# Turning rows feature-major with VectorE in 32x32 blocks, from a quarter-wise DRAM layout, in place of TensorE transposes

## The reference

```
ys = cond / sqrt(512)                                  # (2, 512), one row per batch
d  = rsqrt((ys*ys) @ (weight*weight) + 1e-8)
xf = ((x * ys[:, None, :]) @ weight) * d[:, None, :]   # (4096, 512)
top1   = argmax(softmax(xf @ gate_w.T))                # expert 0 or 1 for each token
shared = relu(xf @ sw1 + sb1) @ sw2 + sb2              # hidden size 2048
routed = sum over e of (relu((xf * onehot_e) @ w1[e] + b1[e]) @ w2[e] + b2[e])
out    = x + routed + shared
```

## Time and profile before

| | |
|---|---|
| median of 3 runs | 1588.66 us |
| profiled execution, span from first to last instruction | 1588.7 us |
| PE busy | 1577.0 us (99%) |
| DVE, ACT, POOL busy | 630.3, 348.1, 156.9 us (40%, 22%, 10%) |
| granted TensorE clock, mean | 0.996 of full speed |
| DMA | 105.65 MB, 67 GB/s in the mean |
| `rows` load of 1 MB (L338, L316), issue to landing | 7.0 us median of 8 |
| xf store of 256 KB (L304), issue to landing | 2.0 us median of 32 |

### The profile page before, as it was taken

One profiled execution on the slowest core, in us unless ns is written; L12 is line 12 of the kernel. 1 busy time (PEld: TensorE's weight loads), 2 busy tenths in 40 slices (PEclk: granted clock), 3 DMA queues, 4 the chain that ended last, 5 costly groups with the idle time before them and its releaser, 6 DMA issues.

```text
span 1588.7 us, 23419 instructions
## 1 busy us (share of the span) xinstructions
PE 1577.0 (99%) x8516; PEld 1365.6 (86%) x8516; DVE 630.3 (40%) x1349; ACT 348.1 (22%) x644; POOL 156.9 (10%) x204
## 2 busy tenths in 40 slices
PE   8999999999999999999999999999999999999998
PEld 7878888888888888888889999999999999999997
DVE  6885532323232323323257333333337333333333
ACT  3443211111111111111134111111125111111112
POOL 0000620000000000000010111111111111110112
PEclk8999999999999999999999999999999999999999
DMA  5655230202010020202034111110016111000111
GB/s 187 218 184 168 85 95 14 93 13 92 13 61 31 13 92 13 92 13 80 14 126 146 33 40 40 40 40 26 26 44 206 40 40 40 30 24 26 40 40 43
DMA packets 51458, 105.65 MB, mean 67 GB/s; under 512 B 6433, under 2 KB 6945, under 8 KB 51425
## 3 DMA queue, kind: packets, MB, share of 16 engines
q1 hardware_dynamic: 41888, 77.90, 14.8%
q0 software_dynamic: 9536, 27.32, 5.6%
HBM read 79.48 MB, written 26.25 MB: 67 GB/s over the span
## 4 chain that ended last, share of the span: by engine, by line
PE 97%; issue 1%; DMA 0%; DVE 0%; POOLq 0%; POOL 0%; ACT 0%; DVEq 0%; ACTq 0%; SPq 0%
PE h_ps L1074 45%; PE y_ps L1091 44%; PE h_ps L1007 6%; PE t_ps L1053 2%; PE h_ps L981 0%; POOLq L422 0%; DMA res<-partial_scratch,idx_res 0%; PE y_ps L996 0%; PE y_ps L1159 0%; DMA stage<-w_pack 0%; PE t_ps L987 0%; PE y_ps L987 0%; POOL out L444 0%; PE t_ps L1194 0%; PE h_ps L1133 0%
## 5 line engine op out<-in xcount | busy, mean ns | idle before, releaser
L1074 PE MATMUL h_ps<-x_hi,w_hi 128*128 128x256 f32 (+1 forms) x1536 | 488.6, 318 | 1.6 <-DVE x_lo L739 1.5
L1074 PE MATMUL h_ps<-x_hi,w_lo 128*128 128x256 f32 (+1 forms) x1536 | 489.0, 318 | 0.0
L1074 PE MATMUL h_ps<-x_lo,w_hi 128*128 128x256 f32 (+1 forms) x1536 | 488.9, 318 | 0.0
L563 ACT ACTIVATE hf<-h_ps,b 128x256 f32<-128x256 f32 (+1 forms) x384 | 210.3, 548 | 1116.8 <-PE h_ps L1074 1116.6
L903 DVE CAST h_hi<-hf 128x256 fp32r<-128x256 f32 (+1 forms) x384 | 134.3, 350 | 806.0 <-ACT hf L563 804.5
L1091 PE MATMUL y_ps<-w_hi,h_hi 128*128 128x512 f32 x1024 | 404.0, 395 | 0.0
L1091 PE MATMUL y_ps<-w_lo,h_hi 128*128 128x512 f32 x1024 | 400.9, 392 | 0.0
L1091 PE MATMUL y_ps<-w_hi,h_lo 128*128 128x512 f32 x1024 | 398.7, 389 | 0.0
L1074 PEld LDWEIGHTS h_ps<-x_hi,w_hi 128*128 128x128 f32 x1536 | 291.7, 190 | 32.3 <-issue 2.2
L1074 PEld LDWEIGHTS h_ps<-x_lo,w_hi 128*128 128x128 f32 x1536 | 291.8, 190 | 28.8 <-issue 0.2
L1074 PEld LDWEIGHTS h_ps<-x_hi,w_lo 128*128 128x128 f32 x1536 | 291.7, 190 | 20.0
(11 more groups left out here) (132 smaller groups left out, 733.8 us busy)
## 6 DMA issues: line engine op xcount, KB each, us to landing
stage<-w_pack SPq DMA_DIRECT2D x96, 256.0 KB, 2.8
res<-x_cols SPq DMA_DIRECT2D x32, 256.0 KB, 2.8
xf_scratch<-hf SPq DMA_DIRECT2D x32, 256.0 KB, 2.0
rows<-xf_scratch SPq DMA_DIRECT2D x8, 1024.0 KB, 7.0
res<-x_rows SPq DMA_DIRECT2D x8, 1024.0 KB, 5.3
scratch<-w_pack SPq DMA_DIRECT2D x16, 512.0 KB, 3.6
partial_scratch<-res SPq DMA_DIRECT2D x32, 256.0 KB, 2.2
rows<-w_cond SPq DMA_DIRECT2D x4, 256.0 KB, 4.7
```

Source lines behind the costliest of these rows:

```text
L563: nc.scalar.activation(hf[:, j % 2, 0:tok], h_ps[j % 2][:, 0:tok], ACT.Relu, bias=b1[:, ffn, j:j + 1]).then_inc(hf_ready, 1)
L1074: last = nc.tensor.matmul(h_ps[j % 2][:, 0:tok], lhs[:, j, part], rhs[:, k, 0:tok], start=(k == 0 and q == 0), stop=(k == KD - 1 and q == 2))
```

## The change

`xf_dram` now has four times as many rows of 128 features: row q * 4096 + t has, of token t, block q of each of the four 128-feature pieces (the columns of the projection's weights and of the gate's are reordered on the host, so the kernel's own result comes out in this order). `rows` is filled so that 32 partitions hold quarter q and each partition has 32-token blocks behind one another: a wide slot takes four loads of 32 partitions, a narrow slot eight indirect DMAs of 128 rows of 512 bytes instead of two of 2048 bytes. VectorE turns all 32x32 blocks in place with one transpose instruction (`flip`: 128 x 2048 elements for a wide slot, 128 x 1024 for a narrow one), after step j = 13 of the slot ahead, after quad 2 in a short slot, and in the prologue ahead of the last round of tiles. ScalarE and VectorE then make `x_hi` and `x_lo` from `rows` in SBUF. All transposes at L1053 and L1180 are gone. A second table of token numbers, with q * 4096 added, is read by four DMAs of 32 partitions. What frees `rows` for the next load or gather is now `x_lo` (`xt_lo`) and no longer the transpose (`xt_ps`).

```diff
@@ layout and loads
-    xf_dram = nc.dram_tensor("xf_scratch", (N, D), F32).ap()
+    xf_dram = nc.dram_tensor("xf_scratch", (QD * N, QF), F32).ap()
-        rows = sb("rows", [P, M, D])
+        rows = sb("rows", [P, JW, QF])
-                    sp.dma_start(token_rows(xf_dram, c * P, P), xo[:, i % 2, :]).then_inc(xf_out[i % 2], DMA)
+                    sp.dma_start(quads_of(c * P, P), xo[:, i % 2, :].rearrange("p (q f) -> p q f", q=QD)).then_inc(xf_out[i % 2], DMA)
-                sp.wait_ge(xt_ps, KD * (s + 1))
-                sp.dma_start(rows[:], slot_rows(xf_dram, s + 1)).then_inc(rows_in, DMA)
+                sp.wait_ge(xt_lo, KD * (s + 1))
+                for q in range(QD):
+                    sp.dma_start(rows[q * B32:(q + 1) * B32, :, :], quad_rows(q, s + 1)).then_inc(rows_in, DMA)
@@ GpSimd
+                for q in range(QD):
+                    pool.dma_start(tab_rows[q * B32:(q + 1) * B32, :],
+                                   table_dram.rearrange("(c p) w -> p c w", p=B32)[:, :, 0]).then_inc(tab_dma, DMA)
-                wait_apart(pool, xt_ps, until(s, NARROW, KD, KD // 2), tab_ready)
-                numbers(idx_rows, tab_in, s)
-                for m in range(ME):
-                    pool.indirect_dma_start(rows[:, m, :], None, xf_dram,
-                                            bass.IndirectOffsetOnAxis(idx_rows[:, m:m + 1], 0)).then_inc(rows_gathered, DMA)
+                wait_apart(pool, xt_lo, until(s, NARROW, KD, KD // 2), tab_ready)
+                numbers(idx_rows, tab_rows, s, JN)
+                for j in range(JN):
+                    pool.indirect_dma_start(rows[:, j, :], None, xf_dram,
+                                            bass.IndirectOffsetOnAxis(idx_rows[:, j:j + 1], 0)).then_inc(rows_gathered, DMA)
@@ ScalarE, per slot
-                for f in range(KD // per_bank):
-                    act.wait_ge(xt_ps, until(s, kind, KD, KD // 2) + f + 1)
-                    nc.scalar.copy(x_hi[:, f * per_bank:(f + 1) * per_bank, 0:tok],
-                                   bank(s, f)[:].rearrange("p (k n) -> p k n", k=per_bank)).then_inc(xt_hi, 1)
+                act.wait_ge(xt_flip, s + 1)
+                for k in range(0, KD, per):
+                    nc.scalar.copy(by_block(x_hi, k, k + per, 0, tok), turned(k, k + per, 0, tok // B32)).then_inc(xt_hi, 1)
@@ VectorE
+            def flip(s, kind):
+                if kind is WIDE:
+                    dve.wait_ge(rows_in, QD * DMA * (s + 1))
+                else:
+                    dve.wait_ge(rows_gathered, JN * DMA * (s - SHARED + 1))
+                blocks = rows[:, 0:kind[1] // B32, :]
+                nc.vector.transpose(blocks, blocks).then_inc(xt_flip, 1)
+            flip(0, WIDE)
             tiles_round(ROUNDS - 1, True, False)
+                    if j == 13:
+                        flip(s + 1, nxt)
+                    if u == QUADS - 2:
+                        flip(s + 1, NARROW)
@@ TensorE
-                transpose(s + 1, nxt, range(0, 2))
                 down(s, ffn, HC - 3, kind)
-                if banks > 2:
-                    transpose(s + 1, nxt, range(2, banks))
                 down(s, ffn, HC - 2, kind)
-                pe.wait_ge(hf_ready, HC * (s + 1))
-                transpose(s + 1, NARROW, range(0, 2))
                 down4(QUADS - 1)
-            for m in range(M):
-                for k in range(KD):
-                    last = nc.tensor.transpose(bank(0, m)[:, k * P:(k + 1) * P], rows[:, m, k * P:(k + 1) * P], ident[:])
@@ host
+    quads = np.arange(D).reshape(KD, QD, B32).transpose(1, 0, 2).reshape(D)
-        "w_cond": lay(w_cond.reshape(KD, P, D).transpose(1, 0, 2)),
+        "w_cond": lay(w_cond[:, quads].reshape(KD, P, D).transpose(1, 0, 2)),
-        "gate": lay(gate),
+        "gate": lay(gate[:, quads]),
```

More of the change, by code:

```diff
@@ L60 @@
 PAD = N
+QD = 4
+B32 = P // QD
+QF = D // QD
+JW = T // B32
+JN = TE // B32
 EPS = 1e-8
@@ L167, in build @@
         tab_in = sb("tab_in", [P, COLS], I32)
[L168 removed]
+        idx_rows = sb("idx_rows", [P, JN], I32)
         idx_res = sb("idx_res", [P, ME], I32)
         idx_out = sb("idx_out", [P, ME], I32)
[L172 removed]
+        w_raw = rows[:, :, :].rearrange("p (k j) f -> p k (j f)", k=KD)
         ring = res
         xo = hf
+        tab_rows = soft[:, :, :].rearrange("p a t -> p (a t)")[:, 0:QD * COLS].bitcast(I32)
         junk = bias[:, 1, :]
@@ L315, in _ @@
             sp.wait_ge(wc1_ready, KD)
-            sp.dma_start(rows[:], slot_rows(xf_dram, 0)).then_inc(rows_in, DMA)
+            for q in range(QD):
+                sp.dma_start(rows[q * B32:(q + 1) * B32, :, :], quad_rows(q, 0)).then_inc(rows_in, DMA)
             with sp.Fori(ROUNDS // 2, ROUNDS - 1) as t:
@@ L413, in _, with numbers @@
                 pool.dma_start(tab[:], table_dram.rearrange("(c p) w -> p c w", p=P)[:, :, 0]).then_inc(tab_dma, DMA)
[L414 removed]
+                for q in range(QD):
+                    pool.dma_start(tab_rows[q * B32:(q + 1) * B32, :],
+                                   table_dram.rearrange("(c p) w -> p c w", p=B32)[:, :, 0]).then_inc(tab_dma, DMA)
+            pool.wait_ge(tab_dma, (1 + QD) * DMA)
             pool.tensor_scalar(tab_in[:], tab[:], N - 1, None, ALU.min).then_inc(tab_ready, 1)
[L417 to L421 removed]
+            for q in range(QD):
+                pool.wait_ge(tab_ready, 1 + q)
+                part = slice(q * B32, (q + 1) * B32)
+                pool.tensor_scalar(tab_rows[part, :], tab_rows[part, :], N - 1, q * N, ALU.min,
+                                   ALU.add).then_inc(tab_ready, 1)
+            pool.wait_ge(tab_ready, 1 + QD)
+            def numbers(dst, table, s, n=ME):
+                pool.tensor_copy(dst[:], columns(table, (s - SHARED) * n, n))
                 pool.drain()
             def gather_rows(s):
[L426 to L430 removed]
+                wait_apart(pool, xt_lo, until(s, NARROW, KD, KD // 2), tab_ready)
[3 more added lines that the diff above has]
+                                            bass.IndirectOffsetOnAxis(idx_rows[:, j:j + 1], 0)).then_inc(rows_gathered, DMA)
             def gather_res(s):
@@ L470, in _ @@
             pool.wait_ge(scattered, ME * DMA * EXPERT)
-            pool.wait_ge(rows_gathered, ME * DMA * (EXPERT + 1))
+            pool.wait_ge(rows_gathered, JN * DMA * (EXPERT + 1))
         @block.scalar
@@ L775, in transposed @@
             def transposed(s, kind):
[L777 to L783, removed]
+                per, tok = kind
+                for k in range(0, KD, per):
+                    dve.wait_ge(xt_hi, until(s, kind, KD, KD // 2) + k // per + 1)
+                    nc.vector.tensor_tensor(by_block(x_lo, k, k + per, 0, tok), turned(k, k + per, 0, tok // B32),
+                                            by_block(x_hi, k, k + per, 0, tok).bitcast(F32), ALU.subtract).then_inc(xt_lo, 1)
             r = [0]
@@ L1037, in _ @@
                     project(t, i, 1)
[L1039 to L1054, removed]
             def hidden(s, ffn, j, kind):
@@ L1093, in down, with slot @@
                 last.then_inc(y_mm, 1)
-            def slot(s, ffn, nxt):
+            def slot(s, ffn):
                 kind = WIDE if ffn == 0 else NARROW
@@ L1196, in _ @@
             with pe.Fori(SHARED, end0) as s:
-                slot(s, 1, NARROW)
+                slot(s, 1)
             s1 = pe.snap(t0 + SHARED)
@@ L1201, in _ @@
             with pe.Fori(s1, end1) as s:
-                slot(s, 2, NARROW)
+                slot(s, 2)
             with pe.If(end1 < SLOTS):
```

36 lines of the change are left out of this document (19 added, 17 removed).

## The result

| | before | after |
|---|---|---|
| median | 1589.73 us (4 runs, 1588.6 to 1591.39) | 1579.36 us (4 runs, 1577.19 to 1582.9) |
| ratio, 95% interval | | 0.9932 [0.9915, 0.9949] |
| profiled span | 1588.7 us | 1577.1 us |
| granted clock, mean | 0.996 | 0.992 |
| DVE, POOL busy | 630.3, 156.9 us | 669.2, 271.5 us |

The change makes the kernel 0.68% faster; 1577.8 was forecast. The profiled run took 1578.81 us, so its span lies 1.7 us under its time. The same holds before the change: a run of 1590.34 us there had a span of 1588.6. That the profiled span before was the same number as the median of three runs was chance, and a forecast of the time should have added 1.7 us to the span. The working is compared on the spans: 1588.7 and 1577.1, a gain of 11.6, where 10.9 was forecast.

The account below looks back on a forecast made before the run. The prediction took TensorE to bound the kernel, with 97% of the chain of waits. Transposes, last slot (two terms), ordinary narrow slots, slot 16, prologue: 1588.7 - 27.8 + 7.8 + 2.7 + 1.0 + 3.4 + 2.0 = 1577.8 us; range 1567 to 1592.

Parts of the forecast that it names:

- Transposes: TensorE: 30 groups of eight at L1053 and two at L1180 leave the chain, 27.8 us won.
- The block transpose: VectorE: 1.2 us narrow, 2.3 us wide, under 4.9 us of free time in a narrow slot; 0 on the path.
- The handover: Start of the next narrow slot: x_lo is ready with 1.4 us of cover, so 0 on the path.
- Gathers: GpSimd: six more indirect DMAs per narrow slot at 1.3 us each, everything behind them 7.8 us later.
- Ordinary narrow slots: Slots 9 to 15 and 17 to 23: VectorE stalls some 4 us for res; +1 us in all (0 to 4).
- The last slot: res lands 7.8 us later, in full on the chain; the last 12 matmuls at the 1.2 GHz level add 2.7 us.
- Slot 16: Late res delays the exchange of weights, so hidden(11) starts late: +3.4 us (3.0 to 3.8; 0 to 7 if otherwise).
- Prologue: The load of rows in 512-byte pieces delays x_cols where no cover is left: +2.0 us (0 to 9.9).
- Rival 1: GpSimd's list reaches TensorE in every narrow slot, from 1.44 to 1.54 us a gather; about 1611 us at 1.73; 12%.
- Rival 2: The prologue is bound by DMA, pieces of 512 bytes costing 103 ns each: +36, about 1612 us; 5%.
- Rival 3: Late res costs less: shorter drain, clock stays up, slot 16 and prologue absorb their delays; 1568 us; 15%.
- Rival 4: The transposes were hidden anyway and nothing is won; 1599 us; 2%.

Follow-up runs that it names:

- experiment 5: Kernel after, with VectorE's block transpose done three times in each slot from 1 on instead of once; 1576.87 us, ratio to before 0.9914.
- experiment 6: Kernel after, with VectorE's block transpose done five times in each slot from 1 on instead of once; 1620.76 us, ratio to before 1.019.
- experiment 4: Kernel after, with twelve gathers of rows in each narrow slot instead of eight; 1633.48 us, ratio to before 1.027.
- experiment 7: Kernel after, with the prologue's four loads of rows issued one by one behind every second x load instead of together; 1575.48 us, ratio to before 0.9904.
- experiment 8: Kernel after, with wide slots' loads of rows going to all 128 partitions instead of 32, result wrong; 1576.72 us, ratio to before 0.9913.
- experiment 9: Kernel after, with the edits of experiment 1 and experiment 7 together; 1563.3 us, ratio to before 0.983.
- experiment 1: Kernel after, with GpSimd gathering res before the next slot's rows and no block transpose for a slot after the last; 1567.37 us, ratio to before 0.9845.

## Why the prediction was right

The time came out at 1579.4 against 1577.8, by the mechanism forecast: 30 groups of transposes leave the chain, and the extra gathers give back a third of it in the last slot. That the number is so close is luck in part, as the sum of the errors below shows. Term by term, in the profiled execution:

- **Transposes, -27.8.** Right. The ordinary slots lost 0.87 for each group, and the wide ones a little more: 1.83 for two.
- **The block transpose, 0.** Right in price (1.2 and 2.3 forecast, 1.24 and 2.31 measured; the prediction's other estimates for a narrow slot, 2.5 and 4.9, were too high), cover (4.9 forecast, about 5.0) and sign; experiments 5 and 6 show the cover from both sides.
- **The handover, 0.** Right: hidden(0) waits for nothing in the ordinary slots.
- **Gathers, 1.3 us each.** Right, 1.28 in the mean (1.25 median, 1.31 before).
- **Ordinary narrow slots, +1.0.** It was 0. `res` landed 25.6 us after the slot's start, not 26.4 to 27.2, mostly since the wait ahead of the first gather of `res` is shorter behind small gathers, 2.45 us where it was 3.14 in slot 20. The median landing of a gather of rows went from 3.5 us to 2.6. The limit itself held (experiment 4).
- **The last slot, +7.8 + 2.7.** It was 6.5 + 1.8. Of the 1.3 too many in the first, 0.9 is the shorter drain and wait behind the small gathers (2.86 us; 3.79 before the change), 0.2 the landing of `res` (4.06; 4.30). In the second the clock was at its low level for the first matmuls only, not for all twelve.
- **Slot 16, +3.4.** It was 4.5 (slots 15 and 16 together took 3.6 more, with one counted group of 0.87 gone from them). VectorE waits 4.32 us for `res` there, within the forecast, and the wait for the weights is 1.88, not 3.4. Two things that I hadn't in the working make up for it. The slot opens with a wait of 1.76 us for `hf`, where 0.87 of transposes had stood, and behind the 1.88 the clock fell (granted 0.50 from 1205.3 on):

```profile
1203.78 0.38 PE L1099 MATMUL h_ps<-x_hi,w_hi 128*128 128x256 f32 x1 [1.88 <-DVE w_lo L744]
...
1205.33 0.63 PE L1116 MATMUL y_ps<-w_hi,h_hi 128*128 128x512 f32 x1
1205.76 0.63 PE L1116 MATMUL y_ps<-w_lo,h_hi 128*128 128x512 f32 x1
```

  1.88 + 0.9 + some 1.8 for matmuls 0.43 us apart instead of 0.23 is the 4.5. The sign of one hole of 3 to 4 us was wrong by this: there are two of under 2 us. In experiments 5, 7 and 8, which have the same list on GpSimd, `hf` is waited for 0.6 to 1.6 us and the weights 2.0 to 3.1, the clock falls each time, and slot 16 takes 49.9 to 51.6 us (50.8 here, 46.3 before): 3.7 to 5.3 more. `hf` is late because ScalarE stands ahead of it at the rounding of weights that haven't landed: it waits 2.35 and 1.09 us for `stage` there, in experiment 9 2.23 us alone.
- **Prologue, +2.0.** The mis-sized term: it was 4.0 in this execution (slot 1 began 0.5 later, with four groups of transposes, 3.5 us, gone ahead of it; experiment 7 has slot 0 at 107.42, here it began at 111.63). The hole is 2.01 us, just as forecast, but its price is twice its length, since the clock fell to the 1.2 GHz level behind it: nine matmuls, up to 0.2 us longer each. In the last slot I had priced this, in the prologue and slot 16 not. It is no fixed price, though. Of the six executions with this prologue the clock fell in two; in experiment 4, with a hole of 1.95 us and no fall, slot 1 began 2.2 us earlier, and the forecast 2.0 would have been right.

The errors cancel: 2.0 too little in the prologue and 1.1 in slot 16, against 2.2 too much in the last slot, 1.0 in the ordinary ones and 0.5 in the wide, which leaves the 0.7 between 10.9 and 11.6. Another execution gives another sum: without the fall of the clock in the prologue the gain would have been some 1.6 us larger (an estimate from experiment 4's slots). The four runs of the kernel after go from 1577.19 to 1582.9 us. Rival 1 (GpSimd's list reaches TensorE) fell by the price of a gather, 1.28 against the 1.44 it needed. That VectorE's casts hold GpSimd up isn't seen either: beside them the gathers of slot 20 start 1.25 to 1.32 us apart. Experiment 4 shows that its mechanism is real and begins between eight and twelve gathers; with 2.7 us left in slot 20, by the third extra one (an estimate). Rival 2 (prologue bound by DMA) fell: 24 to 50 us the share went from 0.64 to 0.71 at the same 203 GB/s, which is 29 us of the engines for 9.5 tiles x 384 more pieces, some 8 ns each and not 103. Rival 3 was right on the ordinary slots and the drain, and lost in the prologue and slot 16. Rival 4 fell with the table above.

## What to carry to other kernels

Work that leaves the chain is won in full only if what replaces it isn't ahead of something late on another engine's list. Here a swap of two lines in GpSimd's loop, with a transpose for no slot left out, gave as much again as the whole change. Price a hole of 2 us or so on TensorE between its length and about twice that, because in some executions the clock falls behind it, which cost 1.6 us here, and in others it doesn't; so compare more than one execution before a microsecond is given a cause. And of an in-order list ask what its last round does: here it served a slot that doesn't exist, ahead of the last stores.

## What the runs showed of the hardware

- VectorE's transpose of 32x32 blocks on 4-byte elements costs what the elementwise passes (0.43 us for 128x256, 0.69 for 128x512) give for its size: 1.24 us for 128x1024 and 2.31 us for 128x2048, 1.04 ns an element. It works in place.
- An indirect DMA of 128 rows costs GpSimd nearly the same from start to start whatever the row: 1.30 us with 64 bytes, 1.25 with 512 bytes (median of the kernel after), 1.31 with 2 KB; a few take up to 1.8.
- Behind holes of TensorE of about 2 us the clock falls to the 1.2 GHz level in some executions only. It fell behind 1.84 us (slot 16, experiment 1), 1.88 and 2.01 (slot 16 and prologue, kernel after) and behind 8 of the 14 holes of 2.4 to 3.0 us in experiment 4. It did not behind 1.95 (prologue, experiment 4), 2.70 (slot 16, experiment 6) and the other 6 of the 14, nor, from 24 us on, behind any hole of 1.76 us or less.
- A piece of 512 bytes costs some 8 to 9 ns of a DMA engine over what its bytes cost, in stores from and loads into 128 partitions, and 36 ns in loads into 32.
- Behind four loads of rows into 32 partitions, 2048 such pieces, one of SyncE's next issues of a load of x took 1.83 us instead of 0.35 (1.0 to 1.6 in five other executions). With the same pieces going to 128 partitions the longest was 0.83; with one such load at a time the issues took 0.50 to 0.76 (experiments 7 and 9).
